# A state-space and expert kernel on one core: norm sums in four row groups, the norm chain and the weight splitting placed earlier in each turn, and the first transpose ahead of the chunk products

## The reference, cut to what matters

```python
Bm = rmsnorm((x @ WB.T).reshape(B_, L, H, N), Bn_w) + B_bias     # H = 64 heads, N = 128
Cm = rmsnorm((x @ WC.T).reshape(B_, L, H, N), Cn_w) + C_bias
theta_cumsum = jnp.cumsum((x @ Wth.T).reshape(B_, L, H, N // 2) * dt[..., None], axis=1)
Bm, Cm = rope(Bm, theta_cumsum), rope(Cm, theta_cumsum)
# for each token t, with the weights alpha, beta, gamma of dt and lam
h = at * h + bt * outer(B_prev, x_prev) + gt * outer(Bt, xt)
yt = einsum(Ct, h)
```

## Time and profile before

| | |
|---|---|
| median of 3 runs | 3599.38 us (3589.8 to 3600.61) |
| the profiled execution, its own time | 3601.3 us |
| its span in the trace | 3599.5 us |
| mean granted TensorE clock, share of full speed | 0.882 |
| busy share of the span | PE 81%, DVE 66%, ACT 51%, POOL 43% |

### The profile page before, as it was taken

How to read it: one execution, slowest core, us unless ns; L and a number is a source line. 1 busy time by engine, 2 the same in 40 slices (tenths; PEclk the granted TensorE clock), 3 DMA queues, 4 the chain that set the end, 5 groups by cost and what they waited for, 6 DMA issues and landing times.

```text
span 3599.5 us, 84310 instructions
## 1 busy us (share of the span) xinstructions
PE 2897.9 (81%) x28752; PEld 2199.6 (61%) x28752; DVE 2374.4 (66%) x3926; ACT 1820.9 (51%) x3740; POOL 1539.4 (43%) x1420
## 2 busy tenths in 40 slices
PE   5139957788888899999977999999899998279573
PEld 4128846466666657667654667676676676168462
DVE  5214224699999849889945988884888885243135
ACT  1016624566666356666614666663666672046331
POOL 3550050255555416655610555551455553510345
PEclk7559968889899899999978999998999998589785
DMA  9537755466665246556403666642666653467564
GB/s 387 197 123 254 255 163 179 142 183 184 177 184 176 77 139 171 164 162 171 134 3 119 173 172 172 171 134 68 170 172 171 172 160 115 158 206 254 175 205 138
DMA packets 311258, 605.54 MB, mean 168 GB/s; under 512 B 59136, under 2 KB 159616, under 8 KB 310016
## 3 DMA queue, kind: packets, MB, share of 16 engines
q1 hardware_dynamic: 286464, 535.63, 48.9%
q0 software_dynamic: 24576, 67.14, 5.6%
HBM read 446.25 MB, written 155.32 MB: 167 GB/s over the span
## 4 chain that ended last, share of the span: by engine, by line
PE 53%; DVE 19%; issue 10%; another core or an unknown queue 7%; ACT 4%; DMA 4%; POOL 1%; DVEq 1%; SPq 1%; POOLq 0%; ACTq 0%
PE bank L63 15%; PE bank L568 7%; PE bank L1327 4%; DVE tmp L1275 3%; PE bank L1197 3%; PE bank L1393 3%; DVE xbc L1251 3%; DMA rc_in<-decay_t 3%; PE bank L581 2%; PE bank L559 2%; PE bank L1391 2%; PE cs_sn L581 2%; PE bank L1367 2%; DVE rot L1275 2%
## 5 line engine op out<-in xcount | busy, mean ns | idle before, releaser
L63 PE MATMUL bank<-xh,wb 128*128 128x512 f32 x2048 | 685.4, 416 | 73.1 <-ACT btr L1342 43.2
L644 DVE TENSOR_TENSOR hh<-sg,bank 128x96 f32<-128x96 f32 x384 | 97.5, 254 | 596.4 <-ACT sg L619 372.6
L63 PEld LDWEIGHTS bank<-xh,wb 128*128 128x128 f32 x2048 | 373.3, 192 | 190.4 <-ACT btr L1342 63.9
L1206 ACT ACTIVATE xbc<-bank,norm_w 128x512 f32<-128x512 f32 x512 | 350.7, 685 | 240.8 <-PE bank L63 234.1
L1295 POOL TENSOR_TENSOR sq<-cst,rho 128x512 f32<-128x512 f32 x128 | 133.5, 1043 | 742.8 <-DVE xbc L1251 411.3
L1283 POOL TENSOR_TENSOR rot<-rot,tmp 128x512 f32<-128x512 f32 x256 | 341.8, 1335 | 238.3 <-DVE tmp L1275 238.3
L568 PE MATMUL bank<-wgu,xgT 128*128 (+1 forms) x1536 | 343.7, 350 | 107.6 <-issue 68.2
L63 PE MATMUL bank<-xl,wb 128*128 128x512 f32 x1024 | 408.5, 399 | 0.0
L1284 POOL TENSOR_TENSOR rot<-rot,tmp 128x512 f32<-128x512 f32 x256 | 358.7, 1401 | 0.0
L568 PEld LDWEIGHTS bank<-wgu,xgT 128*128 128x128 f32 x1536 | 261.0, 204 | 118.5 <-issue 118.1
L1275 DVE SCALAR_TENSOR_TENSOR rot<-xbc,bias,cs_sn 128x1024 f32<-128x1024 f32 x256 | 325.4, 1271 | 8.4 <-DVE xbc L1251 6.8
(11 more groups left out here) (277 smaller groups left out, 6084.7 us busy)
## 6 DMA issues: line engine op xcount, KB each, us to landing
wb<-watt_dram SPq DMA_DIRECT2D x96, 1024.0 KB, 7.7
rr_bc<-rr_dram SPq DMA_DIRECT2D x128, 512.0 KB
yd<-ys SPq DMA_DIRECT2D x96, 512.0 KB
wd<-w_down SPq DMA_DIRECT2D x384, 96.0 KB
watt_dram<-wb SPq DMA_DIRECT2D x32, 1024.0 KB, 5.4
dt_bc<-row_dram SPq DMA_DIRECT2D x256, 128.0 KB
al_bc<-row_dram SPq DMA_DIRECT2D x256, 128.0 KB, 3.2
xd<-xg SPq DMA_DIRECT2D x12, 2048.0 KB, 23.7
```

The costliest lines, as they stand in the source:

```text
L63: ins = e.matmul(dst, a, m, start=start and c == 0, stop=stop and c == n - 1, skip_group_check=not (start and stop))
L1206: e.activation(xbc[j % 4][:, i, :], of(i)[:, :], ACT.Copy, scale=norm_w[:, i:i + 1])
```

## The change

It has six parts.

1. **Sums of squares.** `ss_pe` writes eight products of 256 columns into four groups of 32 rows of `SSB` (0, 32, 64, 96), where it wrote four products of 512 columns into two groups. The first half of the tokens is in rows 0 to 63, the second in rows 64 to 127.
2. **Norm chain.** `R_act` therefore reads 100 x 256 where it read 36 x 512, into a tile of its own. `R_sp1` and `R_sp2` issue two transfers each where they issued one.
3. **Place of the chain.** In `turn_act`, `R_act` stands ahead of `T_act2`. In `turn_sp`, `R_sp1` stands ahead of the loads of `dt_bc`, `end_bc`, `th` and `wb`; it stood behind them.
4. **Weight parts (first scan).** `wb_high_act` and `th_high_act` stand ahead of `K_act` and no longer behind `A_act` of part 1; `wb_low_dve` and `th_low_dve` stand ahead of `F_dve3` and no longer behind it. The angle weights are split one turn later than before, and their raw load stands at the end of SP's turn.
5. **First transpose.** `tr_pe` of the first half stands ahead of `G_pe`.
6. **Its wait.** It waits for `e_Rb`, which `F_pool` raises after the B type, and no longer for `e_R`.

```diff
-        stdr = decay_t[0:36, :, :, :].rearrange("p k q a -> p (k q a)")
-        NORM_ROWS = slice(28, 36)
+        HALF = SEQ // 2
+        stdr = sb("stdr", [100, HALF])[:, :]
+        NORM_ROWS = [slice(28, 36), slice(92, 100)]
...
             for eo in range(2):
-                for ty in range(2):
-                    first = 30 - 28 * (1 - ty) - 2 * (j % 2)
-                    ins = e.matmul(SSB[32 * ty:32 * ty + 32, :], one_hot[:, first:first + 32], sq4[:, 2 * ty + eo, :],
-                                   start=j % 2 == 0 and eo == 0, stop=j % 2 == 1 and eo == 1, skip_group_check=True)
+                for half in range(2):
+                    for ty in range(2):
+                        first = 30 - 28 * (1 - ty) - 2 * (j % 2)
+                        g = 64 * half + 32 * ty
+                        ins = e.matmul(SSB[g:g + 32, 0:HALF], one_hot[:, first:first + 32], sq4[:, 2 * ty + eo, half * HALF:(half + 1) * HALF],
+                                       start=j % 2 == 0 and eo == 0, stop=j % 2 == 1 and eo == 1, skip_group_check=True)
...
-            e.activation(stdr, SSB[0:36, :], ACT.Sqrt, scale=1.0 / NS, bias=eps_nm[0:36, 0:1]).then_inc(e_sr.sem, 1)
+            e.activation(stdr, SSB[0:100, 0:HALF], ACT.Sqrt, scale=1.0 / NS, bias=eps_nm[0:100, 0:1]).then_inc(e_sr.sem, 1)
...
-            e.dma_start(rc_in[:, :], stdr[NORM_ROWS, :].rearrange("r (c w) -> r c w", w=32)).then_inc(a_r1.sem, 16)
+            for h in range(2):
+                e.dma_start(rc_in[CL * h:CL * h + CL, :], stdr[NORM_ROWS[h], :].rearrange("r (c w) -> r c w", w=32)).then_inc(a_r1.sem, 16)
...
-            e.dma_start(rr_dram[par].rearrange("r (c w) -> (r c) w", w=32), rc[:, :]).then_inc(a_r2.sem, 16)
+            for h in range(2):
+                dst = rr_dram[par][:, h * HALF:(h + 1) * HALF].rearrange("r (c w) -> r c w", w=32)
+                e.dma_start(dst, rc[CL * h:CL * h + CL, :]).then_inc(a_r2.sem, 16)
...
+                if ty == 0:
+                    ins.then_inc(e_Rb.sem, 1)
...
-                e.wait_ge(e_R.sem, e_R.at(p + 1))
+                e.wait_ge(e_Rb.sem, e_Rb.at(p + 1))
...
                 if K:
+                    tr_pe(e, p, jp, 0, 0)
                     G_pe(e, p, jp)
-                    tr_pe(e, p, jp, 0, 0)
...
+                if RG:
+                    R_act(e, gm + 1)
                 if T:
                     T_act2(e, n + 1, j + 1)
-                if RG:
-                    R_act(e, gm + 1)
+                if is_first(b) and not last:
+                    wb_high_act(e, q + 4, j, it * 2 + j // 2 + 2)
+                if is_first(b) and not (last and j >= 2):
+                    th_high_act(e, q + 2, j, it * 2 + j // 2 + 1)
...
                 if RG:
                     R_dve(e, gm + 1)
+                if is_first(b) and not last:
+                    wb_low_dve(e, q + 4, j)
+                if is_first(b) and not (last and j >= 2):
+                    th_low_dve(e, q + 2, j)
                 F_dve3(e, n, j, q, [0])
...
-                if is_first(b) and not (last and j >= 2):
-                    th_store_sp(e, q + 2, j)
+                if is_first(b) and not (first and j == 0) and not (last and j == 3):
+                    th_store_sp(e, q + 1, j + 1)
+                if RG:
+                    R_sp1(e, gm + 1)
...
-                if not (last and j >= 1):
+                if not is_first(b) and not (last and j >= 1):
...
-                if RG:
-                    R_sp1(e, gm + 1)
...
+                if is_first(b) and not (last and j >= 1):
+                    th_load_sp(e, b, q + 3, j + 1)
```

More of the change, by code:

```diff
@@ L1211, in R_act @@
             e.wait_ge(e_ssm.sem, e_ssm.at(2 * (gm + 1)))
-            e.wait_ge(a_r1.sem, a_r1.at(gm))
-            e.activation(stdr, SSB[0:36, :], ACT.Sqrt, scale=1.0 / NS, bias=eps_nm[0:36, 0:1]).then_inc(e_sr.sem, 1)
+            e.wait_ge(a_r1.sem, a_r1.at(2 * gm))
+            e.activation(stdr, SSB[0:100, 0:HALF], ACT.Sqrt, scale=1.0 / NS, bias=eps_nm[0:100, 0:1]).then_inc(e_sr.sem, 1)
         def R_dve(e, gm):
-            e.wait_ge(a_r1.sem, a_r1.at(gm + 1))
-            e.wait_ge(a_r2.sem, a_r2.at(gm))
+            e.wait_ge(a_r1.sem, a_r1.at(2 * (gm + 1)))
+            e.wait_ge(a_r2.sem, a_r2.at(2 * gm))
             e.reciprocal(rc[:, :], rc_in[:, :]).then_inc(e_rc.sem, 1)
@@ L1231, in R_sp2 @@
             e.nop(nofuse=True)
-            e.dma_start(rr_dram[par].rearrange("r (c w) -> (r c) w", w=32), rc[:, :]).then_inc(a_r2.sem, 16)
+            for h in range(2):
+                dst = rr_dram[par][:, h * HALF:(h + 1) * HALF].rearrange("r (c w) -> r c w", w=32)
+                e.dma_start(dst, rc[CL * h:CL * h + CL, :]).then_inc(a_r2.sem, 16)
         def R_sp3(e, gm, par):
-            e.wait_ge(a_r2.sem, a_r2.at(gm + 1))
+            e.wait_ge(a_r2.sem, a_r2.at(2 * (gm + 1)))
             e.nop(nofuse=True)
@@ L1288, in build @@
         e_own, e_Dp = ev("e_own"), ev("e_Dp")
+        e_Rb = ev("e_Rb")
         def own_pool(e, n, q):
@@ L1487, in turn_act @@
                     e.activation(std[:, 0:1], half_pi[:, 0:1], ACT.Sin)
-                if is_first(b) and not last:
-                    wb_high_act(e, q + 4, j, it * 2 + j // 2 + 2)
-                if is_first(b) and not (last and j >= 1):
-                    th_high_act(e, q + 3, j + 1, it * 2 + (j + 1) // 2 + 1)
                 if A:
@@ L1536, in turn_dve @@
                     gather_turn_dve(e, b, n, q, it, j)
-                if is_first(b) and not last:
-                    wb_low_dve(e, q + 4, j)
-                if is_first(b) and not (last and j >= 1):
-                    th_low_dve(e, q + 3, j + 1)
                 if K:
@@ L1593, in pairs_pe @@
             Y_pe(e, p - 1, j - 1, (b + 1) * (NP // 2) - 1)
+            tr_pe(e, p, j, 0, 0)
             G_pe(e, p, j)
-            tr_pe(e, p, j, 0, 0)
             z_pe(e, b, 2)
@@ L1608, in pairs_act @@
             if is_first(b):
-                th_high_act(e, 2, 0, 1)
                 wb_high_act(e, 3, 1, 1)
@@ L1639, in pairs_dve @@
             T_dve2(e, N, 0)
-            if is_first(b):
-                th_low_dve(e, 2, 0)
             if is_first(b):
```

## The result

The changed kernel takes 3686.51 us (median of 4, 3680.14 to 3710.03) against 3594.59 us before (median of 4): a ratio of 1.027 (95% interval 1.022 to 1.032). The time grew, as forecast, but by 92 us or 2.7%, where 0.4% was forecast, and it lies above the range of 3540 to 3655 us. The profiled execution has a span of 3681.0 us, 81.5 more than before. By the distance from a scan's first `T_dve1` to its last, 3.7 of these came in the first scan, 21.9 in the second, 29.4 and 29.5 in the third and fourth; all that lies outside the scans took 3.0 less.

The account below looks back on a forecast made before the run. It took the loop through the norm chain's transfers to bound the changed kernel's scans 2 to 4, and DVE the first. 3601.3 + 35 - 14 - 7 = 3615 us, so 3613 to be measured; range 3540 to 3655.

Parts of the forecast that it names:

- the pace that the loop sets: Scans 2 to 4: double turns (two turns) of 31.3 us, against 31.0 in scan 2 and 30.1 after: +35 us.
- the ends of the scans: First and last turns of each scan: PE's 0.87 us less counts in some four turns a scan, -14 us.
- the first scan: DVE bound: shorter low parts give -2.2 us a double turn, ACT's waiting +1.7; -7 us over 14 double turns.
- The mechanism: Norm chain: `wb` now precedes the store of the reciprocals, so `F_dve1` of even turns waits some 3 us for `rr_bc`.
- the loop's length: From one even turn's `F_dve1` to the next, through roots, `wb` and `rr_bc`: 31.2 us, bounds 28.4 to 33.
- There PE's 0.87 us counts: Ends of the scans: the sums' 0.87 us less on PE each turn shortens some four turns a scan, -14 us.
- the fast rival of 3480 us: Engines set the pace: double turns of 27.6 us in scans 3 and 4, 28.4 in scan 2; all faster cases 0.3.
- Costs at most that where DVE is ahead: First transpose ahead of `G_pe`: DVE gets the chunk products 0.55 us later, at most that cost where DVE is ahead.
- The low parts: First scan, DVE, at their new place: 2.7 us for both together, 1.1 us less a turn; bounds 1.6 to 3.8.
- ACT's wait for the raw load: First scan, even turns: ACT waits 3.2 us ahead of the high part, of which 1.7 us reach DVE.
- The 5.3 us of the roots: Kernel before: the roots' 16 KB took 5.3 us because SP's transfers leave in order, behind the 1 MB `wb` load.

Follow-up runs that it names:

- b_chain_early: The kernel before with only the norm chain's place changed (part 3) and a tile of its own for the roots: 3669.46 us, 1.016.
- a_roots_late: The changed kernel with `R_sp1`, the spreading of the roots, put back behind the row and weight loads: 1.005 of before.
- b_sums_four: The kernel before with only the sums of squares in four row groups and their two transfers each, all at the old places: 1.004, repeated 1.005.
- b_recip_mid_later: The kernel before with weight parts ahead, their raw load ahead of the store, and the reciprocal between the two types' products in scans 2 to 4 only: 0.978.
- the filler run: `b_sums_four` plus eight zero-weight passes a turn: 1.014, inconclusive; with them in scans 2 to 4 only: 1.007, against 1.005 without them on the same chip.
- b_transpose_first: The kernel before with only parts 5 and 6, the first transpose ahead of the chunk products and its finer wait: 1.010, +39 us.
- b_load_roots_act: The kernel before with weight parts ahead, their raw load ahead of the store, and the roots' transfer `rc_in` issued by ACT: 0.999.
- b_two_each: The kernel before with the roots' and reciprocals' transfers as two of 64 partitions each, sums and places as before: 1.0018, 5 us.
- b_recip_mid: The kernel before with weight parts ahead, their raw load ahead of the store, and the reciprocal between the two types' products in all scans: 1.004.

## Why the prediction was wrong, and where it was right

- **Where the 68 us are.** The profiled execution took 3682.7 us, the sum of the prediction 3615. Of the difference 43 us are the pace that the loop sets, 17 the ends of the scans, 11 the first scan, and -3 all that lies outside.
- **The mechanism was right.** The 1 MB load entered the chain, `rr_bc` was late, and `F_dve1` of even turns waited: `b_chain_early` alone loses 59 us by it, and `a_roots_late` gets scans 3 and 4 back from 486 to 458 us.
- **The step that failed first is the loop's length, mis-sized by 0.8 us.** Its terms, forecast and measured as medians of the third scan: `F_dve1` to the roots 10.3 and 10.4; roots to the issue of `wb` 5.1 and 5.8 (the two root transfers and the way to the next issue hold SP for 1.77 us, not 1.2); `wb` to the issue of `rr_bc` 8.9 and 8.3; from there to `F_dve1` 6.9 and 7.5. Sum 32.0, not 31.2. By the pace the scans lost about 72 us in 36 double turns, 78 in the 39 of the forecast, against +35. Of these 43 us more the 0.8 us make 31; most of the rest is scan 2, whose mean double turn is 32.8 us though its median loop is 32.1.
- **"There PE's 0.87 us counts" was wrong.** The ends of the scans were to give 14 us; what lies outside those 36 double turns grew by about 9 us in scans 2 to 4. `b_sums_four`, which left the chain in place, gained nothing. The second step that failed is this price: it reads a PE that is 95% busy as the bound of scans 2 to 4. DVE's odd turn hangs on the chain (`b_recip_mid_later` shortened it with PE's work unchanged), PE waits for DVE's state scan instead, and the filler run shows a pace that hardly follows PE's busy time. So the fast rival of 3480 us didn't come even where the load was out of the loop (`a_roots_late`, 1.005).
- **"Costs at most that where DVE is ahead" was wrong for the first transpose.** The sentence named a price (0.55 us a turn; in `b_transpose_first` the first scan is 0.7 us a turn longer) and then counted it nowhere, not even in the first scan, where DVE was said to be the bound. By itself the part cost 39 us, 22 of them there; in the whole change the first scan shows little of it.
- **The first scan.** The low parts measured 1.22 and 1.26 us, together 2.5 where 2.7 was taken. ACT's wait for the raw load was 58.9 / 13 = 4.5 us, not 3.2, and PE's clock fell from 0.91 to 0.86. It came out 3.7 us longer, not 7 shorter.
- **The 5.3 us of the roots** were given a cause, the order of SP's transfers, that `b_load_roots_act` contradicts: 6.4 us on another queue beside the load, 3.4 at most where it isn't in flight. The forecast didn't rest on it: the early roots passed ahead of `wb`, by any queue.

The ratios of the parts add up, but the lengths of single scans don't: the parts' first scans are together 30 us longer than before's, that of the whole change 3.7. Nor does undoing match doing: `a_roots_late` takes 2.2% off, `b_chain_early` puts 1.6% on. Parts 4 and 5 may cover each other in the first scan, which is 538.8 us long in `a_roots_late` with both; they were not tried as a pair.

## What to carry to other kernels

When a small transfer's wait is moved away from a large load, ask which later step of the same chain the large load now precedes, and add up that loop from issue to issue. It came out right to 0.8 us in 32 here, and even that is 31 us over 39 double turns, so check each term that changes (here the two issues in place of one). A busy share of 95% doesn't make an engine the bound. Before pricing work taken from it, look for a path in the slower of two alternating turns that doesn't touch it; and price an order's cost on every engine in every stage, above all where that engine is the bound. A wait for a transfer that can't be made faster is best filled with work that stands behind it, as long as the loop has room.

## What the runs showed of the hardware

- A wait of PE of 1.8 us, with the engine 64% busy in the microsecond ahead of it, was followed by 6 to 7 us at a granted clock of 0.50 (`b_sums_four`).
- A transfer of 16 KB on another engine's queue took 6.4 us with 1 MB in flight, no less than the 5.3 behind it on the same queue, and at most 3.4 without it (`b_load_roots_act`).
- On some chips the kernel before took 3600 us and on others 3355. Most of that lies outside the scans: the span of `b_two_each` on a chip of the second kind was 241 us below that of the kernel before on one of the first, and its four scans together 9 us. For the faster code of `b_recip_mid`, scans 2 to 4 differ by 28 us between the kinds.
